# Mixing the second relational layer's matrices: which engine does which unit, and when its chunks are loaded

## The chip, the core and the metric

The kernel runs on one core of a Trainium2 chip. Its engines work in parallel, each through its own list of instructions, and wait for each other on semaphores: TensorE (PE, matrix products), VectorE (DVE), ScalarE (ACT), GpSimd (POOL), and SyncE (SP), which here only issues transfers. SBUF is the on-chip memory of 128 partitions; PSUM takes TensorE's results. The metric is the time of one execution in microseconds (us).

## What is computed

A graph of 1250 nodes with 512 features goes through four attention and MLP blocks and then through three graph layers. The change touches the last of these parts:

```python
# L1: alpha = x @ wc; beta = x @ wn; mean of beta over neighbours; sum of both
# L2, twice (basis1, then basis2):
def rgcn_gate_layer(x, row, col, edge_type, basis, att, gate_w, root, bias):
    w = jnp.einsum('rb,bio->rio', att, basis)      # att (2, 30), basis (30, 512, 512)
    x_j = x[col]
    for r in range(2):
        gate = jax.nn.sigmoid(x_j @ gate_w[r, :, 0])
        msgs.append(gate[:, None] * x_j @ w[r])
    msg = jnp.where((edge_type == 0)[:, None], msgs[0], msgs[1])
    return segment_sum(msg, row) + x @ root + bias
# L3: two SAGE layers of the same kind
```

The line that matters is the first one: for each of the two relations r, a 512 x 512 matrix is the weighted sum of 30 basis matrices.

## The kernel before

The nodes lie in T = 10 tiles of 125 rows. After the four blocks the kernel is written out by hand, stage by stage, and every engine has the same stages in its program:

- **beta1**: ten products of a node tile with a 512 x 512 matrix (`products`, eight matmuls each), each result split in two pieces by ACT (high part) and DVE (low part, `split_rows`).
- **mean1 / self1**: per tile a gather (`gather`: 20 matmuls of edge counts with all ten tiles' pieces) and one product. DVE adds both to x and takes the tile's statistics. POOL makes the reciprocal deviation (`tile_powers`).
- **msg 0,r** and **agg 0,r** for the relations r = 0, 1 of layer 0: ten products, split as above, then ten gathers. With r = 0 a gather also has the product with the root matrix.
- **msg 1,r** and **agg 1,r** of layer 1, then the SAGE stages.

The products and gathers take turns in five PSUM banks (`POST_BANKS`), so PE can be at most five results ahead of the engine that frees them.

The matrices of layer 1 are mixed while the stages up to `agg 0,1` run. They are w[0] (relation 0) and w[1] (relation 1), called `mixed[1][r]`. The work is cut in 120 units, one for each of 30 bases b and 4 row groups k (u = 4b + k). A unit reads one chunk of 128 x 512 numbers from HBM into a ring of three buffers, `ring[u % 3]`, named basis in the profile. DVE's `mix(n)` does the next n units: two instructions each (L1089, or L1087 for b = 0), accumulator r += att[r, b] * chunk, and then increments `basis_used`. SP's loop at L571 issues chunk n once `basis_used` has reached n - 2. Both queues are in order: a DVE instruction that waits for its chunk holds all that stands behind it, splits and adds included.

Before that loop SP issues the root matrix into w[2] (L560), the coefficients (L561), the two mixed matrices of layer 0 from their place in HBM (L564) and the gate rows (L566). At the same place POOL issues ct2 (L712) and adds a bias to all of x (`add_bias`, L695). Later POOL subtracts ct2 from ct in ten instructions (L719), after which ACT may convert the counts for `agg 0,0`, and adds another bias. PE may not start layer 1 before `mixed_ready`, which DVE gives behind unit 119.

## Time and profile before

| | before |
|---|---|
| median of 3 runs | 3251.54 us (3250.66 to 3256.28) |
| the profiled execution | 3254.82 us |
| its span (first to last instruction) | 3253.1 us |
| PE busy | 2931.6 us, 90% of the span |
| DVE busy | 1850.8 us, 57% |
| POOL busy | 899.4 us, 28% |
| mean granted TensorE clock | 0.952 of full speed |

PE is busy in most of the span, and where it isn't, some other engine or a transfer decides. The stages that the change touches lie between 2437 and 2820 us of the span. The shares over the whole span say little about them, so the views below are of this stretch.

### The profile page before, as it was taken

The page shows a single profiled execution, that of the slowest core. Times are in us where ns is not written, and L with a number is a line of the kernel's source. Part 1 is how long each engine was busy: PE and PEld are TensorE (multiplying, and loading weights), DVE is VectorE, ACT ScalarE, POOL GpSimd, SP SyncE. Part 2 cuts the span into 40 slices and gives each one's busy share as a digit, 9 for nine tenths or more (in the row PEclk, how much of TensorE's full clock was granted, in tenths as well). Part 3 has the DMA queues.
Part 4 walks back from the last instruction along what each step waited for, and adds up shares of the span by engine and source line. Part 5 has one row for each costly group of instructions (what it writes and reads, how often), then busy time and mean ns, then how long its engine had stood idle before and what let it go on. Part 6 is the DMA issues. An engine that isn't in the chain of part 4 may idle for free.

```text
span 3253.1 us, 32006 instructions
## 1 busy us (share of the span) xinstructions
PE 2931.6 (90%) x11830; PEld 1903.3 (59%) x11830; DVE 1850.8 (57%) x3327; ACT 793.8 (24%) x1145; POOL 899.4 (28%) x730
## 2 busy tenths in 40 slices
PE   5978389999899999889999979999977889999999
PEld 1345257777556777546777545777633545566555
DVE  9999345554765554855455764555674888603111
ACT  1154232222221222221222311222311112313221
POOL 6622122334222334221334320334511310000100
PEclk9989689999999999989999999999988989999999
DMA  3000200000310000310000230000144135101001
GB/s 78 1 1 1 93 7 14 1 27 14 107 46 13 1 27 13 95 59 13 1 27 1 67 99 13 1 26 1 51 126 140 51 105 151 52 13 65 13 0 32
DMA packets 69063, 133.70 MB, mean 41 GB/s; under 512 B 10804, under 2 KB 11195, under 8 KB 68908
## 3 DMA queue, kind: packets, MB, share of 16 engines
q1 hardware_dynamic: 63372, 119.62, 12.3%
q0 software_dynamic: 5536, 12.03, 1.1%
q8 instruction: 95, 1.56, 0.2%
q14 instruction: 60, 0.49, 0.1%
HBM read 120.70 MB, written 10.92 MB: 40 GB/s over the span
## 4 chain that ended last, share of the span: by engine, by line
PE 74%; DVE 13%; issue 4%; DMA 3%; DVEq 2%; ACT 1%; POOLq 1%; POOL 1%; SPq 0%; ACTq 0%
PE ps L1484 12%; PE ps L1596 10%; PE ps L1707 9%; PE ps L1736 9%; PE ps L1475 7%; PE ps L1634 4%; PE ps L1569 3%; PE ps L1584 3%; PE ps L1586 3%; PE ps L1587 3%; PE ps L1585 3%; PE ps L1437 2%; PE ps L1728 2%; PE ps L1501 2%; DMA lite_ring<-in_basis 2%
## 5 line engine op out<-in xcount | busy, mean ns | idle before, releaser
L687 POOL TENSOR_TENSOR pacc<-pacc,prob 125x628 f32<-125x628 f32 (+1 forms) x288 | 406.5, 1411 | 383.2 <-DVE prob L1013 383.2
L1484 PE MATMUL ps<-yT,w 128*128 128x416 f32 (+1 forms) x1152 | 438.2, 537 | 15.1 <-DVE qk_lo L957 7.8
L1596 PE MATMUL ps<-prob,big 125*128 125x314 f32 x1280 | 392.6, 428 | 4.6 <-DVE prob L1013 4.6
L966 DVE CUSTOM_DVE_ANT_0 ps<-ps,typed 125x628 f32<-125x628 f32 x320 | 260.1, 823 | 232.4 <-PE ps L1569 232.4
L1307 ACT ACTIVATE prob<-ps 125x628 f32<-125x628 f32 x320 | 221.9, 693 | 632.5 <-PE ps L1587 632.5
L1736 PE MATMUL ps<-pieces,counts_r 125*125 125x512 f32 x1400 | 353.9, 407 | 2.1 <-DVEq L1109 2.1
L1484 PEld LDWEIGHTS ps<-yT,w 128*128 128x128 f32 x1152 | 226.7, 198 | 201.3 <-issue 189.5
L1013 DVE SCALAR_TENSOR_TENSOR prob<-prob,typed 125x628 f32<-125x628 f32 x320 | 259.9, 812 | 124.0 <-ACT prob L1307 124.0
L1736 PEld LDWEIGHTS ps<-pieces,counts_r 125*125 125x125 f32 x1400 | 257.2, 186 | 79.6 <-issue 17.4
L1584 PE MATMUL ps<-qk_hi 128*125 128x314 f32 x640 | 294.9, 461 | 0.0
L1596 PEld LDWEIGHTS ps<-prob,big 125*128 125x128 f32 x1280 | 228.5, 190 | 60.4 <-DVE prob L1013 9.3
L1040 DVE SCALAR_TENSOR_TENSOR lite_acc<-lite_ring,att_w,lite_acc 128x512 f32<-128x512 f32 x232 | 198.7, 898 | 45.0 <-DMA lite_ring<-in_basis 35.7
L651 POOL TENSOR_TENSOR rstd<-var,mhalf 125x1 f32<-125x1 f32 x110 | 70.2, 639 | 547.2 <-DVE var L919 547.0
L957 DVE SCALAR_TENSOR_TENSOR qk_lo<-ps,bcol,qk_hi 128x416 fp32r<-128x416 f32 (+1 forms) x96 | 62.2, 651 | 254.7 <-ACT qk_hi L1269 254.7
L1475 PE MATMUL ps<-w,big 128*125 128x512 f32 x320 | 153.8, 628 | 54.9 <-DVE x L1055 52.0
L1586 PE MATMUL ps<-qk_hi,qk_lo 128*125 128x314 f32 x640 | 198.3, 310 | 0.0
L1587 PE MATMUL ps<-mrow,ones_r 128*125 128x314 f32 x640 | 198.3, 310 | 0.0
L1585 PE MATMUL ps<-qk_lo,qk_hi 128*125 128x314 f32 x640 | 198.1, 310 | 0.0
L683 POOL TENSOR_TENSOR pacc<-prob,zcol 125x628 f32<-125x628 f32 (+1 forms) x32 | 39.3, 1228 | 571.6 <-DVE prob L1013 571.6
L1089 DVE SCALAR_TENSOR_TENSOR w<-basis,att_w,w 128x512 f32<-128x512 f32 x232 | 175.1, 796 | 16.7 <-DMA basis<-in_basis 5.3
L1437 PE MATMUL ps<-onehot_src,onehot_dst 128*125 128x512 f16 x708 | 147.6, 354 | 31.7 <-DVE onehot_src L888 31.4
L1634 PE MATMUL ps<-w,oT 128*125 128x512 f32 x320 | 172.8, 625 | 0.6 <-DVE x L1000 0.6
(210 smaller groups left out, 4612.5 us busy)
## 6 DMA issues: line engine op xcount, KB each, us to landing
lite_ring<-in_basis SPq DMA_DIRECT2D x120, 256.0 KB, 2.6
basis<-in_basis SPq DMA_DIRECT2D x120, 256.0 KB, 2.6
w<-in_m_w SPq DMA_DIRECT2D x8, 1024.0 KB, 6.6
w<-in_wk SPq DMA_DIRECT2D x5, 1024.0 KB, 5.6
oT<-in_cw SPq DMA_DIRECT2D x9, 512.0 KB, 7.7
w<-in_wv SPq DMA_DIRECT2D x4, 1024.0 KB, 5.4
w<-in_wq SPq DMA_DIRECT2D x4, 1024.0 KB, 6.1
w<-in_wo SPq DMA_DIRECT2D x4, 1024.0 KB, 5.4
```

Of the source, the lines that this page charges most:

```text
L687: nc.gpsimd.tensor_tensor(pacc[:, c0:c0 + nn], pacc[:, c0:c0 + nn], prob[:, n % 3, p0:p0 + nn], ALU.add).then_inc(psum_done, 1)
L966: V.tensor_tensor_reduce(out=score_ps(s.slot), in0=score_ps(s.slot), in1=in_quarters(mneg[:, t, c0:c0 + HALF]), scale=1.0, scalar=-BIG, op ...
L1475: last = mm(lin_ps(job, P, D), lhs[:, k, t * P:(t + 1) * P], weight[:, k, :], start=(k == 0), stop=(k == KD - 1))
L1484: last = mm(lin_ps(job, 128, nn), weight[:, k, m * 128:(m + 1) * 128], lhs[:, k, c0:c0 + nn], start=(k == 0), stop=(k == KD - 1))
L1584: mm(o, hi[:, 1, rows], hi[:, 0, cols], start=True, stop=False)
L1585: mm(o, hi[:, 1, rows], lo[:, 0, cols], start=False, stop=False)
L1586: mm(o, lo[:, 1, rows], hi[:, 0, cols], start=False, stop=False)
L1587: last = mm(o, ones_r[:, 0:P], mrow[:, cols], start=False, stop=True)
L1596: last = mm(o_halves[:, b, :], vrow[:, t, h * DH:(h + 1) * DH], prob[:, n % 3, b * QUARTER:(b + 1) * QUARTER], start=(t == 0), stop=(t == ...
L1634: mm(lin_ps(job, P, D), oT[:, t * P:(t + 1) * P], w[0][:, h, :], start=True, stop=True).then_inc(lin_full, 1)
L1707: last = mm(post_ps(job, P, D), lhs[:, k, t * P:(t + 1) * P], weight[:, k, :], start=(k == 0), stop=(k == KD - 1))
L1736: last = mm(post_ps(job, P, D), counts_r[:, slot, k, :], pieces[:, piece, k, :], start=(self_ is None and k == 0 and piece == 0), stop=(k ...
```

## The change

Three things change.

1. **SP's order.** The chunks of the ring come directly behind the coefficients. The gate rows are issued before chunk 6, the two mixed matrices of layer 0 before chunks 10 and 14, the root matrix before chunk 18. On POOL, ct2 is issued when the last product of beta1 is there, behind the first bias.
2. **How many units where.** Per tile: 1 in beta1, 1 in mean1 (was 2), 1 in msg 0,0, 6 in agg 0,0 (was 5), 1 in msg 0,1, 2 in agg 0,1.
3. **Shared units.** In agg 0,0 every second unit (kind S, the others are kind D), and in agg 0,1 every unit, is shared, 50 in all: DVE does relation 0's half alone and increments `basis_used`. POOL then scales the chunk in its ring buffer, in place, and adds it to relation 1's accumulator (`mix_shared`). SP may reuse that buffer when POOL is done (`basis_shared`). DVE waits for POOL where the next whole unit of the same k needs the accumulator. PE waits for all 50 before layer 1.

```diff
+MIX_STEPS = (("beta1", "D"), ("mean1", "D"), ("msg0", "D"), ("agg0", "SDSDSD"), ("msg1", "D"), ("agg1", "SS"))
+def plan_mix():
+    units, shared = [], {}
+    for name, kinds in MIX_STEPS:
+        for t in range(T):
+            for kind in kinds:
+                if kind == "S":
+                    shared[len(units)] = len(shared) + 1
+                units.append(name)
+    return units, shared
...
             sp.wait_ge(blk_done, 2)
-            sp.dma_start(w[2][:], a["wk"][BLOCKS].rearrange("(k p) n -> p k n", p=128)).then_inc(root_in, 16)
             sp.dma_start(att_w[:].rearrange("p r b -> p (r b)"), a["att"][2 * BASES:].partition_broadcast(128)).then_inc(att_in, 16)
-            sp.wait_ge(mixed_out, 16 * BLOCKS)
-            for r in range(2):
-                sp.dma_start(mixed[0][r], mixed_d[r, :, :].rearrange("(k p) n -> p k n", p=128)).then_inc(mixed_in, 16)
-            sp.wait_ge(gate_rows_out, 64)
-            sp.dma_start(gate_row[0], gate_rows_d[0, :, :].partition_broadcast(P)).then_inc(gate_rows_in[0], 16)
             for n in range(BASES * KD):
                 b, k = n // KD, n % KD
+                if n == 6:
+                    sp.wait_ge(gate_rows_out, 64)
+                    sp.dma_start(gate_row[0], gate_rows_d[0, :, :].partition_broadcast(P)).then_inc(gate_rows_in[0], 16)
+                if n in (10, 14):
+                    r = (n - 10) // 4
+                    sp.wait_ge(mixed_out, 16 * BLOCKS)
+                    sp.dma_start(mixed[0][r], mixed_d[r, :, :].rearrange("(k p) n -> p k n", p=128)).then_inc(mixed_in, 16)
+                if n == 18:
+                    sp.dma_start(w[2][:], a["wk"][BLOCKS].rearrange("(k p) n -> p k n", p=128)).then_inc(root_in, 16)
                 if n >= 3:
                     sp.wait_ge(basis_used, n - 2)
+                    if n - 3 in SHARED:
+                        sp.wait_ge(basis_shared, SHARED[n - 3])
                 sp.dma_start(ring[n % 3][:], a["basis2"][b, k * 128:(k + 1) * 128, :]).then_inc(basis_in[n % 3], 16)
...
+            def mix_shared(name):
+                for u in (u for u in SHARED if MIX_AT[u] == name):
+                    b, k = u // KD, u % KD
+                    pool.wait_ge(basis_in[u % 3], 16 * (u // 3 + 1))
+                    pool.wait_ge(basis_used, u + 1)
+                    acc = mixed[1][1][:, k, :]
+                    nc.gpsimd.tensor_scalar(ring[u % 3][:], ring[u % 3][:], att_w[:, 1, b:b + 1], None, ALU.mult)
+                    nc.gpsimd.drain()
+                    nc.gpsimd.tensor_tensor(acc, acc, ring[u % 3][:], ALU.add)
+                    nc.gpsimd.drain().then_inc(basis_shared, 1)
...
-            nc.gpsimd.dma_start(ct2[:], count_rows(ct2_d)).then_inc(ct2_in, 16)
             pool.wait_ge(post_in, 16)
             add_bias(brow, 0, T)
+            pool.wait_ge(post_full, g["beta1"][-1].full)
+            nc.gpsimd.dma_start(ct2[:], count_rows(ct2_d)).then_inc(ct2_in, 16)
...
             add_bias(brow, 2, 2 * T)
+            mix_shared("agg0")
             late_load(w[2][:], matrix("root2"), g["agg", 0, 0][-1], pw_in)
             pool.wait_ge(agg_ready, 1)
             nc.gpsimd.dma_start(gate_row[1], gate_rows_d[1, :, :].partition_broadcast(P)).then_inc(gate_rows_in[1], 16)
+            mix_shared("agg1")
...
                     dve.wait_ge(basis_in[u % 3], 16 * (u // 3 + 1))
-                    for r in range(2):
+                    earlier = [SHARED[v] for v in range(k, u, KD) if v in SHARED]
+                    if u not in SHARED and earlier:
+                        dve.wait_ge(basis_shared, earlier[-1])
+                    for r in range(1 if u in SHARED else 2):
...
-                mix(1)
                 tile_shift(POST_NORM[NORM2], t)
...
-                        mix(5)
+                        mix(6)
...
                     pe.wait_ge(mixed_ready, 1)
+                    pe.wait_ge(basis_shared, len(SHARED))
```

The order of the instructions shows it at three places. First SP's transfers from the end of the four blocks on, before the change:

```order
L557 DMA mixed_d<-lite_acc 128x2x512
L560 DMA w<-in_wk 128x4x512
L561 DMA att_w<-in_att 128x60
L564 DMA big<-mixed_d 128x4x512 x2
L566 DMA big<-gate_rows_d 125x1024
L571 DMA basis<-in_basis 128x512 x120
```

And with the change (the loop's line is now L594):

```order
L575 DMA mixed_d<-lite_acc 128x2x512
L578 DMA att_w<-in_att 128x60
L594 DMA basis<-in_basis 128x512 x6
L583 DMA big<-gate_rows_d 125x1024
L594 DMA basis<-in_basis 128x512 x4
L587 DMA big<-mixed_d 128x4x512
L594 DMA basis<-in_basis 128x512 x4
L587 DMA big<-mixed_d 128x4x512
L594 DMA basis<-in_basis 128x512 x4
L589 DMA w<-in_wk 128x4x512
L594 DMA basis<-in_basis 128x512 x102
```

The big transfers have moved from ahead of the first chunk to between the first 18 chunks. Second, DVE in two successive tiles of agg 0,0, before:

```order
L1159 TENSOR_TENSOR agg<-ps,brow 125x512
L1089 SCALAR_TENSOR_TENSOR w<-basis,att_w,w 128x512 x10
L1159 TENSOR_TENSOR agg<-ps,brow 125x512
L1089 SCALAR_TENSOR_TENSOR w<-basis,att_w,w 128x512 x10
L1106 SCALAR_TENSOR_TENSOR pieces<-ps,gate,pieces 125x512
```

And with the change:

```order
L1198 TENSOR_TENSOR agg<-ps,brow 125x512
L1129 SCALAR_TENSOR_TENSOR w<-basis,att_w,w 128x512 x9
L1198 TENSOR_TENSOR agg<-ps,brow 125x512
L1129 SCALAR_TENSOR_TENSOR w<-basis,att_w,w 128x512 x9
L1146 SCALAR_TENSOR_TENSOR pieces<-ps,gate,pieces 125x512
```

A tile now has nine mixing instructions for six units where it had ten for five. Third, POOL from the subtraction of ct2 on, before:

```order
L719 TENSOR_TENSOR typed<-typed,ct 125x1250 x10
L695 TENSOR_TENSOR x<-x,brow 125x5120
L701 DMA w<-in_root 128x4x512
L724 DMA brow<-gate_rows_d 125x1024
L701 DMA w<-in_W_l 128x4x512
```

With the change the same place begins as follows, and the last two of these rows (one unit) come 30 times before the next transfer:

```order
L754 TENSOR_TENSOR typed<-typed,ct 125x1250 x10
L718 TENSOR_TENSOR x<-x,brow 125x5120
L738 TENSOR_SCALAR basis<-basis,att_w 128x512
L740 TENSOR_TENSOR w<-w,basis 128x512
```

POOL had nothing to compute between the second bias and the end of the layer. Now it has 100 instructions of 128 x 512 numbers there, 60 of them in agg 0,0, and each unit's second one reads what the first wrote.

## Rows read from the trace of the kernel before

**Rows 1.** The page's head line.
```profile
span 3253.1 us, 32006 instructions
```

**Rows 2.** The chain that ended last, 2250 to 3254: start, us, what.
```profile
2441.88 28.96 DMA basis<-in_basis
...
2578.69 28.14 POOLq L720
```

**Rows 3.** Timeline of PE, 2430 to 2500: start, us, line; in brackets idle before.
```profile
2438.97 13.90 PE L1707 MATMUL ps<-agg,yT 128*125 128x512 f32 x32
2472.77 15.95 PE L1707 MATMUL ps<-agg,yT 128*125 128x512 f32 x32 [19.91 <-DVE pieces L1103]
...
2495.82 3.60 PE L1707 MATMUL ps<-agg,yT 128*125 128x512 f32 x8
```

**Rows 4.** Timeline of DVE in beta1.
```profile
2470.93 0.88 DVE L1087 TENSOR_SCALAR w<-basis,att_w 128x512 f32<-128x512 f32 x2 [27.69 <-DMA basis<-in_basis]
...
2489.73 0.69 DVE L1103 TENSOR_TENSOR pieces<-ps,pieces 125x512 fp32r<-125x512 f32 x1
...
2492.09 0.69 DVE L1103 TENSOR_TENSOR pieces<-ps,pieces 125x512 fp32r<-125x512 f32 x1
```

**Rows 5.** Timeline of SP's transfers at the end of the blocks.
```profile
2437.44 0.46 SPq L560 DMA_DIRECT2D w<-in_wk  x1
...
2441.88 257.11 SPq L571 DMA_DIRECT2D basis<-in_basis  x76
```

**Rows 6.** Timeline of POOL, the two biases.
```profile
2442.76 11.01 POOL L695 TENSOR_TENSOR x<-x,brow 125x5120 f32<-125x5120 f32 x1
...
2606.95 11.00 POOL L695 TENSOR_TENSOR x<-x,brow 125x5120 f32<-125x5120 f32 x1 [0.29 <-issue]
```

**Rows 7.** Timeline of DVE beside POOL's 9.91 us instruction from 2345.68 on.
```profile
2345.75 10.14 DVE L1038 TENSOR_SCALAR lite_acc<-lite_ring,att_w 128x512 f32<-128x512 f32 x1
```

**Rows 8.** DVE's groups by form, 2578 to 2620: count, busy us, mean ns.
```profile
L1089 DVE SCALAR_TENSOR_TENSOR w<-basis,att_w,w 128x512 f32<-128x512 f32 x6 | 15.5, 2624 | 0.3
...
L1106 DVE SCALAR_TENSOR_TENSOR pieces<-ps,gate,pieces 125x512 fp32r<-125x512 f32 x2 | 1.5, 751 | 10.5 <-ACT pieces L1366 10.3
```

**Rows 9.** POOL's L719 alone, 2578 to 2607: min/median/max ns.
```profile
L719 POOL TENSOR_TENSOR typed<-typed,ct x10: 2536/2985/3069, 2578.7 to 2604.1; 125x1250 f16<-125x1250 f16 x10
```

**Rows 10.** POOL's L631 alone (min/median/max), L683 by form, whole span.
```profile
L631 POOL COPY typed<-run x59: 696/978/1218, 140.0 to 338.4; 125x625 int32 x59
...
L683 POOL TENSOR_TENSOR pacc<-prob,zcol 125x628 f32<-125x628 f32 x16 | 19.7, 1232 | 546.9 <-DVE prob L1013 546.9
```

**Rows 11.** Timeline of DVE, first tile of agg 0,0, splits of msg 0,1.
```profile
2643.92 0.69 DVE L1159 TENSOR_TENSOR agg<-ps,brow 125x512 f32<-125x512 f32 x1 [2.98 <-PE ps L1736]
2644.53 7.54 DVE L1089 SCALAR_TENSOR_TENSOR w<-basis,att_w,w 128x512 f32<-128x512 f32 x10
...
2729.91 0.75 DVE L1106 SCALAR_TENSOR_TENSOR pieces<-ps,gate,pieces 125x512 fp32r<-125x512 f32 x1
...
2752.05 0.75 DVE L1106 SCALAR_TENSOR_TENSOR pieces<-ps,gate,pieces 125x512 fp32r<-125x512 f32 x1
```

**Rows 12.** The page's transfers: KB each, us from issue to landing.
```profile
basis<-in_basis SPq DMA_DIRECT2D x120, 256.0 KB, 2.6
```

**Rows 13.** Timeline of DVE, two adds of agg 0,1.
```profile
2771.76 0.69 DVE L1115 TENSOR_TENSOR agg<-agg,ps 125x512 f32<-125x512 f32 x1
...
2777.45 0.69 DVE L1115 TENSOR_TENSOR agg<-agg,ps 125x512 f32<-125x512 f32 x1
```

**Rows 14.** Timeline of PE: agg 0,0 begins, msg 0,1 begins, layer 1 begins.
```profile
2635.64 3.60 PE L1728 MATMUL ps<-w,yT 128*125 128x512 f32 x8
...
2716.49 34.50 PE L1707 MATMUL ps<-big,yT 128*125 128x512 f32 x80
...
2809.83 9.52 PE L1707 MATMUL ps<-w,big 128*125 128x512 f32 x16 [7.53 <-DVEq L1093]
```

**Rows 15.** One stretch: us, busy of PE, PEld, DVE, ACT, POOL, PEclk, DMA share, GB/s.
```profile
2610.00:2618.00 8.00, 6.61 (x8) 2.47 (x8) 7.86 (x2) 2.74 (x5) 7.95 (x1) 0.58 0.00 0
```

More of the change, by code:

```diff
@@ L450, in build @@
         basis_used = sem("basis_used")
+        basis_shared = sem("basis_shared")
         xout_ready = sem("xout_ready")
```

1 line of the change is left out of this document (added).

## The prediction

> **What bounds the kernel now.** I began with the page's head [rows 1] and the chain that ended last, cut to the stretch from 2250 us on. From 2437 us almost every piece of it is PE, with two long strangers [rows 2]: 28.96 us of waiting for the first chunk of the ring, and 28.14 us behind POOL's subtraction of ct2. Then I read the timelines of the engines around each of them.
>
> *Stall A, end of beta1.* PE makes four products in 13.90 us (3.43 us each), stands idle for 19.91 us, and does the last four in 15.95 us [rows 3]. It lacks a PSUM bank, which DVE's second split would free, and DVE stands in the first unit's wait, 27.69 us, until the chunk is there at 2470.93 [rows 4]. SP had issued the root matrix at 2437.44 and four big transfers behind it, and reached the first chunk at 2441.88 [rows 5]. The chunk queued behind some 6 MB, ct2 among them.
>
> *Stall B, msg 0,0.* ACT may not convert counts until POOL has subtracted ct2. The change touches nothing on this path: last add of mean1, statistics, POOL.
>
> *The mixing, agg 0,0 to agg 0,1.* PE needs 8.09 us for a tile of agg 0,0 (2635.64 to 2716.49, ten tiles), while DVE needs 8.27: 0.69 for the add and 7.54 for five units [rows 11, 14]. DVE is 13 us behind when it comes to the first split of msg 0,1 (2729.91). In agg 0,1 it takes 5.69 us per tile [rows 13]. PE begins layer 1 at 2809.83 after a wait of 7.53 us for DVE's last unit [rows 14]. So in this stretch the mixing is the bound, by a little, and whatever it costs more is paid by PE.
>
> **The change, part by part.**
>
> *1. Chunks first: -24.5 us.* SP now reaches chunk 0 about 3 us earlier, ahead of all big transfers. It lands in about 3 us (0.33 for the issue and 2.6 to landing, [rows 12]; SP's issues are short, [rows 5]). DVE isn't free to use it, though. POOL's bias, 11.01 us long [rows 6], starts some 2 us earlier than before, at about 2440.5, since ct2's issue no longer stands ahead of it. DVE's scaling of a chunk can't run beside it: in the blocks the same kind of instruction took 10.14 us beside a long POOL instruction [rows 7]. So unit 0 ends at about 2452.4. The second split follows at 2452.5, just when PE is through with its sixth product (2438.97 + 13.90 = 2452.87). Splits then follow each other every 1.78 us (three units of b = 0: 0.69 + 0.88 + 0.2) and 2.36 us (five later ones, [rows 4]), the last one at 2469.6. PE's four remaining products end at 2453.2 + 13.7 = 2466.9, and its first gather (4.65 us) at 2471.5 instead of 2495.82 to 2496. That is -24.5 us, and the low-clock part of the old restart is in it. The gate rows between chunks 5 and 6, and a mixed matrix ahead of chunk 10, cost nothing: DVE has over a microsecond per product to spare in beta1, and in mean1 there is one unit in 8.5 us. If that cover were gone, each would cost what 1 MB takes beyond a chunk, a few us. ct2 has mean1's 85 us to land in.
>
> *2. One unit less per tile of mean1: 0.* PE bounds mean1. DVE's idle time there grows. Stall B stays as it is, only 24.5 us earlier.
>
> *3. agg 0,0 with shared units: +41 us.* By DVE's own work the tile would be cheap: 0.69 + 3 x 0.77 + 3 x 1.53 = 7.6 us, below PE's 8.09. What decides is the loop around the three buffers. Follow four units from an S half on DVE:
> - POOL makes its part: the scaling, a drain, the add, a drain. The trace has no scaling of 128 x 512 f32. Its copy of 625 numbers took 0.696 at least [rows 10], 0.57 for 512; its two-operand instructions need 2.15 ns a number (11.01 for 5120, [rows 6]), 1.10. I take 0.70, near the copy, since both read one operand. The add: 1.232 for 628 [rows 10] gives 1.00, the bias 1.10, so 1.05. Two drains and the hand-over: no row, 0.15 each and 0.05, between 0 and 0.6 together. Sum 2.10.
> - SP issues the chunk that reuses the buffer, three units on, a D unit: 0.33 + 2.6 = 2.93. Before, three units took 4.6 us per buffer, of which 1.53 for the unit and 2.93 for the load, so there was 0.1 to spare and no wait [rows 11].
> - DVE does that D unit, 1.53, and behind it the next S half, 0.77.
>
> 7.3 us for four units is 11.0 us for the six of a tile. Now the contention. Beside POOL's ten subtractions, DVE's mixing instruction took 2.62 us on average instead of 0.75, while one with an operand in PSUM kept its 0.75 [rows 8]. POOL's own went from 2.536 to 2.985 at the median [rows 9]. So the two take turns, POOL loses 0.45 to each of DVE's, and DVE waits for the rest of POOL's. In the loop POOL's two instructions run while DVE has a D unit, +0.9, and the awaited D unit meets some of POOL's, +0.2 (bounds 0 and 1.75, both its instructions waiting in full; low, since POOL's work for the unit before is then mostly over). 8.4 us for four units, **12.7 us per tile**.
>
> In before's clock, the first split of msg 0,1 then comes at 2643.92 + 127 = 2770.9 instead of 2729.91: +41. The nine splits behind it take 22.1 us before (to 2752.05, [rows 11]) and as long after, PE being five products ahead.
>
> *4. agg 0,1: +1 us.* DVE's own part falls to some 4.2 us and PE needs 5.08. POOL needs 2 x 2.1, and 0.45 for each of the four instructions of DVE (two halves, two logits) that come between: 6.0. I take 5.7 as before, and 1 us for POOL's last unit, for which PE waits now. Bounds -5 (PE decides: 0.6 in each of nine tiles) and +4.
>
> *5. PE's clock: +1 us.* The granted clock was 0.58 while eight matmuls took 6.61 us after stall B [rows 15] (3.43 at full clock). That is the 1.2 GHz level, and PE had been idle. PE will now stand idle for several us before each of the later products of msg 0,1, so one or two of these run slowly, up to 3 us, mostly beneath DVE's splits. The stall that goes in A gives its own slow part back, counted there.
>
> Everything else (POOL's root2, issued behind the 30 units of agg 0,0 but needed only in layer 1; the gate rows of layer 1) has tens of us of cover. The root matrix comes 30 us before its use.
>
> **Sum**: -24.5 + 41 + 1 + 1 = +18.5 on the profiled execution's 3254.8, so 3273. That execution is 3.3 us above the median of the runs shown, so I predict a median of **3270 us**.
>
> **The rivals.** With X for the tile of agg 0,0, the difference is 10X - 86 (the first split) - 24.5 + the last two terms. It changes sign at X = 10.9.
> - *No contention in the loop*: DVE's and POOL's turns fall beside each other by the waits themselves. X is 10.5 (POOL's short ends) to 11.3, and agg 0,1 is bound by PE (-5): -9 to -1, so 3242 to 3250 in the median. For it: both engines wait for chunks a good part of the time. Against: D units are twice as long as the gaps. Chance 0.18.
> - *Faster, the loop is hidden*: POOL's share would have to fit beside the load. PE's pace would need 5.4 us for four units, and load, D unit and S half alone are 5.2. It pays -24.5 and -5.5 in agg 0,1 in full, 3221 us, and it decides wherever X is below 10. For it: DVE's sum of 7.6 us, and 13 us of lag that would be worked off. Chance 0.10.
> - *Every instruction held in full, and POOL slow*: a DVE instruction holds POOL for its whole 0.75, the scaling takes 1.10 and drains 0.3. X is 14.5 to 15, agg 0,1 +5: over +40, so 3291 to 3300. The skill's rule above is on this side, but alone it doesn't reach it. Chance 0.10.
> - *Chunks first brings little*: the bias's 11 us (part 1) is already the price of this; if chunk 0 came only behind the write of lite_acc, it would still land within it. With it shifted by 3 us the sum is +21. Inside the forecast.
>
> **How the numbers follow.** The forecast (X from 11.3 to 14.5, +3 to +40) has 0.62. A measurement tells some 0.2%, 6.5 us, from no change. Of the forecast 0.59 is slower by more, 0.03 within. Of the uncontended case 0.10 is within, 0.08 faster. With the hidden and the slow case: slower 0.69, same 0.13, faster 0.18. The range goes from X = 10.5 to 14.5, 3240 to 3292, and leaves out most of the hidden and of the slow case, 0.18.
>
> **What the profile will show.** PE's idle time at the end of beta1 below 2 us, and DVE's first scaling some 9 us long beside the bias. Adds of agg 0,0 (L1198) 12.7 us apart, DVE waiting for chunks, L1129 on average 0.9 us or more there, POOL's unit 2.9 us from scaling to scaling's end. PE idle for over 30 us in msg 0,1, where it had none. Layer 1 starts about 18 us later. I am wrong if the adds stand under 10.9 us apart, or if POOL's unit takes under 1.8 us in all.

## The result and the profile after

| | before | after |
|---|---|---|
| median of 4 runs | 3253.31 us (3250.66 to 3256.28) | 3298.73 us (3297.8 to 3304.49) |
| the profiled execution's span | 3253.1 us | 3296.1 us |
| POOL busy | 899.4 us | 1048.3 us |
| mean granted TensorE clock | 0.952 | 0.950 |

The ratio after to before is 1.0143, 95% interval 1.0125 to 1.0161: the change makes the kernel 45 us slower. The forecast was 3270 us, with a range up to 3292. The direction came as forecast, and the size lies above the range.

The ratio differs from 1 by more than the noise, though by less than 2%. The two profiled executions are compared stage by stage. The anchor is the start of the third product of beta1, where the long row of products begins: 2438.97 us before [rows 3], 2431.36 after. The change touches nothing that PE waits for ahead of this point, and it still lies 7.6 us earlier in the trace of after. Over all profiled executions of this study it lay between 2430.2 and 2442.5, so executions of one and the same part differ by that much. From the anchor to the end, after takes 864.7 us and before 814.1.

| stretch | before, us | after, us | difference | forecast |
|---|---|---|---|---|
| anchor to the first product of self1 | 56.85 | 32.30 | -24.55 | -24.5 |
| mean1 and self1 | 76.20 | 76.20 | 0 | 0 |
| to the first product of agg 0,0 (stall B in it) | 63.62 | 63.09 | -0.5 | 0 |
| agg 0,0 to the first split of msg 0,1 | 94.27 | 149.19 | +54.9 | +41 |
| the ten splits of msg 0,1 | 22.14 | 22.67 | +0.5 | 0 |
| last split to layer 1 | 57.78 | 78.16 | +20.4 | +1 (and +1 for the clock) |
| layer 1 to the end | 443.3 | 443.1 | -0.1 | 0 |
| sum | | | +50.6 | +18.5 |

Less the 7.6 us ahead of the anchor, that is the +43.0 between the two spans. The forecast is missed by 32 us: 14 of them in the row of agg 0,0, 18 in the one up to layer 1.

**Stall A is gone.** PE in the stretch of [rows 3], on its timeline (start, us, what; idle time before in brackets):

```profile
2431.36 27.82 PE L1746 MATMUL ps<-agg,yT 128*125 128x512 f32 x64
2458.61 5.21 PE L1775 MATMUL ps<-pieces,counts_r 125*125 125x512 f32 x20
2463.66 3.60 PE L1746 MATMUL ps<-agg,yT 128*125 128x512 f32 x8
```

The eight products now run in one piece, where [rows 3] has 19.91 us of idle time behind the first four. DVE's first unit stands on its timeline as

```profile
2435.85 8.41 DVE L1127 TENSOR_SCALAR w<-basis,att_w 128x512 f32<-128x512 f32 x2 [0.21 <-DMA basis<-in_basis]
2444.37 0.69 DVE L1143 TENSOR_TENSOR pieces<-ps,pieces 125x512 fp32r<-125x512 f32 x1
```

and POOL's bias of 11.03 us began at 2432.54. Two scalings that take 0.88 us together elsewhere take 8.41 here and end with the bias. The chunk is there in time, and the second split doesn't hold PE.

**agg 0,0 goes at the pace of the ring.** Its adds on DVE, in one row of the view of that line, and DVE's and POOL's groups of 2611 to 2752 us (count, busy us, mean ns, idle before and its releaser):

```profile
L1198 DVE TENSOR_TENSOR agg<-ps,brow x10: 691/692/694, 2611.2 to 2737.1; 125x512 f32<-125x512 f32 x10
```
```profile
L1129 DVE SCALAR_TENSOR_TENSOR w<-basis,att_w,w 128x512 f32<-128x512 f32 x90 | 82.6, 944 | 51.0 <-DMA basis<-in_basis 48.4
```
```profile
L738 POOL TENSOR_SCALAR basis<-basis,att_w 128x512 f32<-128x512 f32 x30 | 49.6, 1652 | 71.1 <-DVEq L1131 69.8 <-issue 1.3
L740 POOL TENSOR_TENSOR w<-w,basis 128x512 f32<-128x512 f32 x30 | 40.4, 1346 | 4.6 <-issue 4.6
```

Ten adds in 125.9 us are nine intervals of 13.98 us on average (they alternate between some 13 and some 15), where [rows 11] and [rows 14] had 8.27 and 8.09. DVE waits 48.4 us for chunks, and POOL 69.8 us for DVE, of which 27.59 lie ahead of its first unit (2612.80): neither engine is full. What closes the loop stands in the chain that ended last (start, us, what), here one turn of it, and the next one's begin:

```profile
2628.00 1.52 DVE w L1129
2631.21 1.61 POOLq L739
2632.94 1.60 POOLq L741
2634.61 2.54 DMA basis<-in_basis
2637.18 1.59 DVE w L1129
```

DVE's whole unit, the relation-0 half of the next, POOL's scaling and add, then the load into the buffer that POOL gave free, and DVE's next whole unit: 9.18 us for four units, 13.8 for the six of a tile. (Three turns beside it in the same chain took 8.5, 8.7 and 10.4 us. The longest has the add of a tile in it.) Two of POOL's units on its timeline show their parts:

```profile
2616.84 1.56 POOL L738 TENSOR_SCALAR basis<-basis,att_w 128x512 f32<-128x512 f32 x1 [0.27 <-issue]
2618.56 1.28 POOL L740 TENSOR_TENSOR w<-w,basis 128x512 f32<-128x512 f32 x1 [0.15 <-issue]
2622.12 1.56 POOL L738 TENSOR_SCALAR basis<-basis,att_w 128x512 f32<-128x512 f32 x1 [2.29 <-DVEq L1131]
```

**PE pays in msg 0,1 and at the end of agg 0,1.** PE's waits between 2330 and 2880 us (in total, times, longest; of the second row 20.7 us are the two waits in msg 0,0, where before had 19.92):

```profile
PE ps L1746 <- DVE agg L1198: 33.7, 4, 9.3
PE ps L1746 <- DVE pieces L1146: 30.3, 3, 16.6
...
PE ps L1746 <- issue: 16.6, 1, 16.6
PE ps L1576 <- ACT py L1382: 11.2, 6, 1.9
```

Two of the later products of msg 0,1 and the first of layer 1 on PE's timeline:

```profile
2696.68 5.66 PE L1746 MATMUL ps<-big,yT 128*125 128x512 f32 x8 [9.30 <-DVE agg L1198]
2709.88 5.89 PE L1746 MATMUL ps<-big,yT 128*125 128x512 f32 x8 [7.53 <-DVE agg L1198]
...
2852.97 9.44 PE L1746 MATMUL ps<-w,big 128*125 128x512 f32 x16 [16.63 <-issue]
```

PE has finished its ten gathers and stands for 16.63 us. The view names only "issue" for it, but POOL's last add ended 0.15 us before PE went on:

```profile
2851.56 1.26 POOL L740 TENSOR_TENSOR w<-w,basis 128x512 f32<-128x512 f32 x1 [0.15 <-issue]
```

Why that is so late is on POOL's timeline in agg 0,1:

```profile
2813.96 1.81 POOL L738 TENSOR_SCALAR basis<-basis,att_w 128x512 f32<-128x512 f32 x1 [0.27 <-issue]
2815.92 1.29 POOL L740 TENSOR_TENSOR w<-w,basis 128x512 f32<-128x512 f32 x1 [0.15 <-issue]
2817.48 1.72 POOL L738 TENSOR_SCALAR basis<-basis,att_w 128x512 f32<-128x512 f32 x1 [0.27 <-issue]
2819.35 1.51 POOL L740 TENSOR_TENSOR w<-w,basis 128x512 f32<-128x512 f32 x1 [0.15 <-issue]
2821.12 1.80 POOL L738 TENSOR_SCALAR basis<-basis,att_w 128x512 f32<-128x512 f32 x1 [0.26 <-issue]
```

Here POOL never waits for anyone: two units from 2813.96 to 2821.12 are 7.16 us, and DVE's adds of agg 0,1 stand 7.16 us apart as well, where [rows 13] had 5.69. The +20.4 us splits in -0.5 ahead of the first add, +13.3 in the nine intervals, and +7.7 behind the last add. DVE ended its last half at 2846.34, and POOL was nearly two units behind and needed 6.5 us more.

### The profile page after: what moved, and what is told of

Read it like the earlier page. It is cut to its first block, busy times and chain, and to the rows that moved or that the text cites. A ratio compares the mean times of both kernels' runs of the same rounds, so it can differ in the third digit from the quotient of the medians.

```text
span 3296.1 us, 32258 instructions
## 1 busy us (share of the span) xinstructions
PE 2935.7 (89%) x11830; PEld 1901.6 (58%) x11830; DVE 1852.2 (56%) x3277; ACT 793.1 (24%) x1145; POOL 1048.3 (32%) x830
## 4 chain that ended last, share of the span: by engine, by line
PE 72%; DVE 12%; POOLq 4%; issue 4%; DMA 3%; ACT 2%; DVEq 1%; POOL 1%; SPq 0%; ACTq 0%
PE ps L1523 12%; PE ps L1635 10%; PE ps L1746 9%; PE ps L1514 7%; PE ps L1775 7%; PE ps L1673 4%; PE ps L1608 3%; PE ps L1623 3%; PE ps L1625 3%; PE ps L1624 3%; PE ps L1626 3%; PE ps L1476 2%; PE ps L1540 2%; DMA lite_ring<-in_basis 2%; DVE onehot_src L925 2%
## 5 line engine op out<-in xcount | busy, mean ns | idle before, releaser
L1129 DVE SCALAR_TENSOR_TENSOR w<-basis,att_w,w 128x512 f32<-128x512 f32 x182 | 164.7, 934 | 79.0 <-DMA basis<-in_basis 70.3
```

## The experiments

Two theories were set against each other. The first (A): the changed order gains some 24 us by itself, and the shared units lose the rest by the time for which a buffer is held (DVE's half, POOL's unit, load), lengthened by turns at SBUF. The rival: POOL's work in itself, or its contention with DVE, is the cost, and the hold is not. For each run the time from the anchor to the end is given against before's 814.1 us ("by the trace"), besides the medians, since the part ahead of the anchor varies by up to 12 us. "By the trace" is one execution of each kernel. Most stages behind the anchor repeat within 1 us where the program is the same, but not all: from the first product of self1 to the first of agg 0,0 experiments 1 and 11 run the same program and took 140.8 and 145.5 us. There PE's granted clock was 1.00 behind the second split of msg 0,0 in the one and 0.82 in the other. So differences of up to some 5 us by the trace are not shown by it alone. X is the interval of agg 0,0's adds.

**1. The order alone** (e1_chunks_first). All units whole, as many per tile as before:

```diff
-MIX_STEPS = (("beta1", "D"), ("mean1", "D"), ("msg0", "D"), ("agg0", "SDSDSD"), ("msg1", "D"), ("agg1", "SS"))
+MIX_STEPS = (("beta1", "D"), ("mean1", "DD"), ("msg0", "D"), ("agg0", "DDDDD"), ("msg1", "D"), ("agg1", "DD"))
...
                 tile_statistics(t)
+                mix(1)
...
-                        mix(6)
+                        mix(5)
...
-                    pe.wait_ge(basis_shared, len(SHARED))
```

> The new order of the transfers alone (SP's and POOL's), units as before (2 in mean1, 5 in agg 0,0), none shared. Theory A (the order is worth what the two traces show between the third product of beta1 and the first self product, 56.85 us against 32.30, and the loss is all in the shared units): -24.5 us against before, some 3229 us. Theory B (chunks between the big transfers cost something later, in mean1 or at the wait for the mixed matrices): less than 15 us gained.

Measured 3233.44 us against 3250.36, ratio 0.9939 (0.9922 to 0.9956). By the trace -23.8, X = 8.28. The order is worth some 24 us alone (by the ratio 20, from 14 to 25), and nearly all of it, 24.7, stands in the stretch from the anchor to the first product of self1.

**2. The shares with the old order** (e2_old_order). SP's root matrix, mixed matrices and gate rows again ahead of the first chunk, and ct2's issue ahead of the first bias; the rest as in the change.

```diff
             sp.wait_ge(blk_done, 2)
+            sp.dma_start(w[2][:], a["wk"][BLOCKS].rearrange("(k p) n -> p k n", p=128)).then_inc(root_in, 16)
...
+            sp.wait_ge(mixed_out, 16 * BLOCKS)
+            for r in range(2):
+                sp.dma_start(mixed[0][r], mixed_d[r, :, :].rearrange("(k p) n -> p k n", p=128)).then_inc(mixed_in, 16)
```

> The changed kernel with the transfers in their old order: units moved and shared as in the change. Theory A: the two parts add up, so 24.5 us above the changed kernel, some 3323 us (+70 on before). Theory B: the order and the sharing hang together (the gain of the order is partly lost to the later stage, which would have absorbed it), so less than 15 us above the changed kernel.

Measured 3325.72 us, ratio 1.0232 (1.0214 to 1.0249). By the trace +75.0, X = 14.00. The two parts add: -23.8 + 75.0 = +51.2, and the whole change has +50.6.

**3. Units moved, none shared** (e3_units_moved). Six whole units in agg 0,0 and one in mean1:

```diff
+MIX_STEPS = (("beta1", "D"), ("mean1", "D"), ("msg0", "D"), ("agg0", "DDDDDD"), ("msg1", "D"), ("agg1", "DD"))
...
-                    pe.wait_ge(basis_shared, len(SHARED))
```

> New order and the new numbers of units (1 in mean1, 6 in agg 0,0), but every unit whole, made by DVE. Theory A (the sharing costs, not the move): a tile of agg 0,0 is 0.69 + 6 x 1.53 = 9.9 us instead of 8.27, so +16 on the kernel with the order alone: some 3245 us, still below before. Theory B (moving a unit of each tile out of mean1 is what costs): 3275 us or more.

Measured 3240.77 us, ratio 0.9965 (0.9952 to 0.9978). By the trace -10.4, so the unit moved from mean1 costs 13.4 us on top of experiment 1, and that 50 units are shared the other 61. X is 9.80 in seven of the nine intervals and longer in two, 11.04 and 11.70, which stand here as DVE's adds:

```profile
2663.63 0.69 DVE L1198 TENSOR_TENSOR agg<-ps,brow 125x512 f32<-125x512 f32 x1
...
2673.43 0.69 DVE L1198 TENSOR_TENSOR agg<-ps,brow 125x512 f32<-125x512 f32 x1
...
2684.47 0.69 DVE L1198 TENSOR_TENSOR agg<-ps,brow 125x512 f32<-125x512 f32 x1
...
2696.17 0.69 DVE L1198 TENSOR_TENSOR agg<-ps,brow 125x512 f32<-125x512 f32 x1
```
```profile
2687.64 0.83 POOL L724 DMA_DIRECT2D w<-in_root  x1 [99.02 <-PE ps L1775]
```

POOL's 1 MB root matrix was issued at 2687.64 and took 6.3 us to land, so it was coming in during the second of the two, and chunks took up to 5.0 us then. The first lies ahead of it. One chunk took 4.3 us there, and the runs don't show why. The two together are 3.1 of the 13.4 us.

**4. POOL's part left out** (e6_no_pool). Without relation 1's half of the 50 units and all waits for it:

```diff
-                    if n - 3 in SHARED:
-                        sp.wait_ge(basis_shared, SHARED[n - 3])
...
-            mix_shared("agg0")
-            mix_shared("agg1")
...
-                        dve.wait_ge(basis_shared, earlier[-1])
...
-                    pe.wait_ge(basis_shared, len(SHARED))
```

> The changed kernel with POOL's part of the 50 shared units left out (relation 1's matrix lacks these terms), and nobody waits for it: DVE's own sum, with no hold of the buffers and no contention. Theory A: PE decides in agg 0,0 (8.09 us a tile) and in agg 0,1 (5.08), so -24.5 and some -6 more: 3222 us. A rival by which DVE's six units can't run at PE's pace even then, since a half unit leaves the loads too little time (three units in 3.8 us against the 2.93 of a load and 1.53 of a unit): a tile of 8.8 us or more, 3229 us or more.

Measured 3220.69 us, ratio 0.9901 (0.9876 to 0.9925). By the trace -33.8, X = 8.51. For this plan of units this is the floor: 10 us below the order alone. If POOL's work were free, the whole prize would be these 10 us. None of it comes from agg 0,0, where X stays above the 8.28 of experiment 1 and PE's 8.09 that theory A expected, even with no buffer held for POOL. Half of it is agg 0,1, whose adds stand 5.03 us apart instead of 5.58.

**5. POOL without its scaling** (e5_no_scaling). POOL adds the raw chunk.

```diff
-                    nc.gpsimd.tensor_scalar(ring[u % 3][:], ring[u % 3][:], att_w[:, 1, b:b + 1], None, ALU.mult)
-                    nc.gpsimd.drain()
```

> The changed kernel without POOL's scaling of the chunk (relation 1 gets the unscaled chunk): POOL's unit falls from 3.28 us (1.57 + 0.15 + 1.29 + 0.27) to 1.6. Theory A (the length of POOL's part, through the buffer it holds): the loop of four units gets 1.7 us shorter, 2.6 us per tile of agg 0,0, from 14.0 to 11.4, and agg 0,1 falls from 7.16 us per tile to PE's 5.08: about -26 and -20, so 3253 us. Rival (what costs is the turn-taking of DVE and POOL): only half of the 100 turns go, so about -20, 3279 us.

Measured 3259.72 us, ratio 1.0023 (1.0014 to 1.0033). By the trace +6.5, X = 11.25. A unit shorter by 1.8 us takes 2.7 off the tile, 1.5 turns of 1.8. In agg 0,1 the adds stand 6.07 us apart and not 5.08 as expected. That is 9 us in nine intervals, where the run came out 7 us above its expectation.

**6. POOL's work apart from the ring** (e7_pool_apart). In agg 0,0 POOL makes the same two instructions on a buffer of its own, and SP doesn't wait for it:

```diff
+                    scaled = big[:, 4096:4608] if name == "agg0" else ring[u % 3][:]
-                    nc.gpsimd.tensor_scalar(ring[u % 3][:], ring[u % 3][:], att_w[:, 1, b:b + 1], None, ALU.mult)
+                    nc.gpsimd.tensor_scalar(scaled, scaled, att_w[:, 1, b:b + 1], None, ALU.mult)
...
-                    nc.gpsimd.tensor_tensor(acc, acc, ring[u % 3][:], ALU.add)
+                    nc.gpsimd.tensor_tensor(acc, acc, scaled, ALU.add)
```

> In agg 0,0 POOL does its two instructions on a buffer of its own that no transfer writes (relation 1 lacks the chunks of these 30 units), and SP does not wait for it there; agg 0,1 as in the change. POOL's work and its turns with DVE stay, the hold of the chunk's buffer goes. Theory A, revised (the round trip chunk, DVE, POOL, SP, load decides in agg 0,0): the tile falls from 14.0 us to what POOL's three units and DVE's turns need, 10.5 to 11.5, so -25 to -35: some 3268 us. Rival (POOL's throughput with the turns decides in agg 0,0 too): the tile stays at 13 us or more, 3288 us or more.

Measured 3274.66 us, ratio 1.0072 (1.0055 to 1.0088). By the trace +23.4, X = 11.41. POOL's groups in agg 0,0:

```profile
L740 POOL TENSOR_SCALAR big<-big,att_w 128x512 f32<-128x512 f32 x30 | 56.4, 1881 | 37.7 <-DVEq L1133 33.6 <-issue 4.1
L742 POOL TENSOR_TENSOR w<-w,big 128x512 f32<-128x512 f32 x29 | 41.8, 1441 | 4.4 <-issue 4.4
```

The 37.7 us have 27.49 ahead of the first unit. With the hold gone, 2.6 us of X go, and the next bound is near. It is DVE itself, which now hardly waits:

```profile
L1131 DVE SCALAR_TENSOR_TENSOR w<-basis,att_w,w 128x512 f32<-128x512 f32 x90 | 100.9, 1147 | 5.9
```

In the chain that ended last a tile is DVE's nine instructions and its add, and nothing else. The instructions take 1147 ns on average, where experiment 1 has 748, since POOL works beside them nearly without a pause (three units with their gaps are some 11 us of POOL per tile too). So the rival has a part: the turns at SBUF, 3.6 us per tile here, would keep agg 0,0 well above PE's pace even if no buffer were held.

**7. The buffer freed early** (e8_early_free). POOL scales out of the ring into a buffer of its own; SP may reload as soon as that is done.

```diff
+                    scaled = big[:, 4096:4608] if name == "agg0" else ring[u % 3][:]
-                    nc.gpsimd.tensor_scalar(ring[u % 3][:], ring[u % 3][:], att_w[:, 1, b:b + 1], None, ALU.mult)
-                    nc.gpsimd.drain()
-                    nc.gpsimd.tensor_tensor(acc, acc, ring[u % 3][:], ALU.add)
+                    nc.gpsimd.tensor_scalar(scaled, ring[u % 3][:], att_w[:, 1, b:b + 1], None, ALU.mult)
+                    nc.gpsimd.drain().then_inc(basis_scaled, 1)
+                    nc.gpsimd.tensor_tensor(acc, acc, scaled, ALU.add)
```

> The changed kernel, with the scaled chunk of agg 0,0 written to a buffer of its own, so that SP may reuse the ring buffer after the scaling, not after the add. The same arithmetic and instructions. Theory A: the loop of four units gets 1.44 us shorter (0.15 and 1.29), so 2.1 us per tile: -21, some 3278 us. Rival (throughput and turns): no change, 3299 us.

Measured 3278.66 us, ratio 1.0073 (1.0053 to 1.0094). By the trace +24.3, X = 11.57. POOL does all its work here, DVE's instructions are as long as in the change (957 ns), and 2.4 us per tile go with the shorter hold alone. POOL waits 0.75 us for DVE in nearly every unit, so its own pace isn't the bound. That falls against the rival: the work is the same, and only the hold changed.

**8. The second bias behind the mixing** (e9_late_bias). Experiment 1, and:

```diff
-            add_bias(brow, 2, 2 * T)
...
+            pool.wait_ge(mixed_ready, 1)
+            add_bias(brow, 2, 2 * T)
```

The bias behind the subtraction of ct2 now waits for the end of the mixing.

> The order alone, as in e1, and POOL's second bias moved from behind the subtraction of ct2 to the point where the mixing is done. In the trace of the changed kernel DVE's first mixing instruction of msg 0,0 takes 7.7 us beside that bias, and PE waits 4.2 us for the split behind it. If that collision is what holds PE there: 3 to 6 us below e1, some 3225 us. If the bias only collides with other work in its new place: same as e1.

Measured 3229.66 us, ratio 0.9934 (0.9917 to 0.9950). By the trace -26.3, 2.5 below experiment 1, a little less than expected. The wait of PE behind the second split, 3.59 us in experiment 1, is gone in the trace, so the collision was there. That it makes the kernel faster isn't shown: the two ratios can't be told apart, and 2.5 us is within what one execution differs from another there.

**9. The coefficient as a broadcast row** (e10_multiply_by_row). The change, with POOL's scaling as a product of two tensors:

```diff
-                    nc.gpsimd.tensor_scalar(ring[u % 3][:], ring[u % 3][:], att_w[:, 1, b:b + 1], None, ALU.mult)
+                    nc.gpsimd.tensor_tensor(ring[u % 3][:], ring[u % 3][:], att_w[:, 1, b:b + 1].to_broadcast([128, D]), ALU.mult)
```

> The changed kernel with POOL's scaling written as a product of two tensors, the coefficient being broadcast along the row (the same arithmetic). Theory A (POOL's part was mis-sized by its scaling, 1.57 us where the bias, a sum with a broadcast row, took 1.10 for 512 numbers and a sum with a broadcast column 0.95 to 1.0): the scaling falls to 1.0, 0.5 us less in a unit, so 0.8 us per tile of agg 0,0 and 1.0 per tile of agg 0,1: -18, 3281 us. Rival (POOL's second instruction and its turns set the pace, or the form makes no difference): 3299 us.

Measured 3296.17 us, ratio 1.0139 (1.0118 to 1.0160). By the trace +44.3, X = 13.88. A miss: the scaling itself did get shorter, from a median of 1.566 to 1.042 us (view of its line, min/median/max):

```profile
L738 POOL TENSOR_TENSOR basis<-basis,att_w x50: 1040/1042/1599, 2613.7 to 2844.9; 128x512 f32<-128x512 f32 x50
```

But the groups of agg 0,0 show where it went again, DVE's instruction from a mean of 944 ns to 1127 and POOL's add from 1346 to 1460:

```profile
L1129 DVE SCALAR_TENSOR_TENSOR w<-basis,att_w,w 128x512 f32<-128x512 f32 x90 | 99.1, 1127 | 32.4 <-DMA basis<-in_basis 29.7
```
```profile
L740 POOL TENSOR_TENSOR w<-w,basis 128x512 f32<-128x512 f32 x30 | 43.8, 1460 | 4.4
L738 POOL TENSOR_TENSOR basis<-basis,att_w 128x512 f32<-128x512 f32 x30 | 32.9, 1096 | 83.1 <-DVEq L1131 83.1
```

**10. Both** (e11_row_and_free). Experiments 7 and 9 together.

```diff
+                    nc.gpsimd.tensor_tensor(scaled, ring[u % 3][:], att_w[:, 1, b:b + 1].to_broadcast([128, D]), ALU.mult)
+                    nc.gpsimd.drain().then_inc(basis_scaled, 1)
+                    nc.gpsimd.tensor_tensor(acc, acc, scaled, ALU.add)
```

> Both mends at once: the scaling as in e10, and the scaled chunk of agg 0,0 in a buffer of its own as in e8. Theory A: POOL then needs 3 x 2.9 us and the turns in a tile of agg 0,0, about 10.5 us, and 6.2 in one of agg 0,1: some 3259 us, so sharing stays slower than the order alone (3233) even so. Rival (sharing pays once its two costs are mended): 3233 us or less.

Measured 3284.31 us, ratio 1.0096 (1.0078 to 1.0114). By the trace +32.1, X = 12.70: worse than experiment 7 alone, against the expectation. DVE's mean is 1222 ns:

```profile
L1131 DVE SCALAR_TENSOR_TENSOR w<-basis,att_w,w 128x512 f32<-128x512 f32 x90 | 107.6, 1222 | 12.8 <-DMA basis<-in_basis 8.8
```

**11. One shared unit per tile** (e12_one_shared). Experiment 1 with one of five units of agg 0,0 shared. POOL is nearly idle then.

```diff
-MIX_STEPS = (("beta1", "D"), ("mean1", "D"), ("msg0", "D"), ("agg0", "SDSDSD"), ("msg1", "D"), ("agg1", "SS"))
+MIX_STEPS = (("beta1", "D"), ("mean1", "DD"), ("msg0", "D"), ("agg0", "SDDDD"), ("msg1", "D"), ("agg1", "DD"))
```

> The order alone, as in e1 (2 units in mean1, 5 in agg 0,0, 2 in agg 0,1), with only the first of the five units of each tile of agg 0,0 shared. POOL has 3.3 us of work in a tile, so its throughput can't be the bound, and DVE's own sum is 7.6 us. Theory A (the hold of one of three buffers: DVE does two whole units, 3.1 us, while POOL and the load take 3.3 + 2.9): a wait of 3.2 us in every tile, 10.8 us instead of 8.27, so +25 on e1: 3258 us. Rival (only POOL's throughput or the number of turns costs): PE's pace of 8.09 us, 3231 us.

Measured 3260.42 us, ratio 1.0020 (1.0009 to 1.0031). By the trace +10.5, X = 11.42, where all five units whole have 8.28. One tile on DVE's and then POOL's timeline:

```profile
2644.66 0.69 DVE L1199 TENSOR_TENSOR agg<-ps,brow 125x512 f32<-125x512 f32 x1
2645.27 2.71 DVE L1129 SCALAR_TENSOR_TENSOR w<-basis,att_w,w 128x512 f32<-128x512 f32 x3
2648.17 2.44 DVE L1129 SCALAR_TENSOR_TENSOR w<-basis,att_w,w 128x512 f32<-128x512 f32 x2 [0.19 <-issue]
2652.75 1.41 DVE L1129 SCALAR_TENSOR_TENSOR w<-basis,att_w,w 128x512 f32<-128x512 f32 x2 [2.15 <-DMA basis<-in_basis]
```
```profile
2646.21 2.10 POOL L738 TENSOR_SCALAR basis<-basis,att_w 128x512 f32<-128x512 f32 x1 [7.42 <-DVEq L1131]
2648.47 1.59 POOL L740 TENSOR_TENSOR w<-w,basis 128x512 f32<-128x512 f32 x1 [0.15 <-issue]
```

The shared half is done at about 2646.1, POOL at 2650.06, and the chunk that reuses the buffer is there at 2652.75. DVE has used up the other two buffers by 2650.6 and stands for 2.15 us. The two units that it does meanwhile are longer by turns, but they aren't what it waits for. One shared unit per tile costs 3.1 us, 31 in ten tiles, although it takes 0.7 us of work off DVE. The chain that ended last goes through it in every tile: half, POOL's unit, load, then DVE's last two units, add and next half. The expectation had 3.3 us for POOL's unit. It took 4.0 with its drains (2.10 + 1.59 + 0.3), which is the 0.6 us by which X lies above the 10.8 that was expected.

**12. Units where DVE is idle** (e13_idle_units). Experiment 8, with two units ahead of msg 0,1 (behind the gates) and none in the last tile of agg 0,1:

```diff
+            mix(2)
...
-                        mix(2)
+                        mix(2 if t < T - 1 else 0)
```

> e9 (new order, bias behind the mixing, nothing shared) with two units taken from the last tile of agg 0,1 and done behind the gates of layer 0, where DVE waits some 10 us for the counts. Their four instructions take turns with the subtraction of ct2 (3 us each), so the first split comes about 1 us later, and layer 1 starts 3 us earlier: 2 us below e9, some 3228 us. If the waiting time was no real slack: same as e9 or above.

Measured 3228.00 us, ratio 0.9926 (0.9907 to 0.9944). By the trace -25.9 against -26.3: not to be told from experiment 8. Layer 1 starts 5.8 us earlier from the anchor, and the rest takes 6.2 longer. Most of that is one wait: the late bias begins when the mixing is done, and DVE's gate instruction beside it took 11.50 us instead of 0.70. In experiment 8 it did too, but PE didn't wait for what stands behind it. Here DVE's last add of agg 0,1 does, and PE waits 5.25 us:

```profile
2776.50 11.50 DVE L1166 CUSTOM_DVE_ANT_0 ps<-py,brow 125x512 f32<-125x512 f32 x1 [0.25 <-issue]
```
```profile
2790.51 1.09 PE L1579 MATMUL ps<-ident,py 125*128 125x125 f32 x4 [5.25 <-ACT py L1385]
```

So the idle time was real slack, and the late bias took its gain back. Another place for the bias wasn't tried.

**13. POOL only writes** (e14_write_only). In agg 0,0 POOL's two instructions are three fills of a buffer of its own, about as long in all, with the same waits. Relation 1's half is left out there.

```diff
+                    if name == "agg0":
+                        nc.gpsimd.memset(big[:, 4096:5120], 0.0)
+                        nc.gpsimd.drain()
...
+                        nc.gpsimd.drain().then_inc(basis_shared, 1)
+                        continue
```

> The changed kernel; in agg 0,0 POOL's part of a shared unit is three settings of 128 x 1024 numbers to zero, each with its drain, in a region that nobody reads (relation 1 lacks these units): estimated 3.3 us, about the length of the real part, but POOL reads no SBUF. Everything waits as in the change. Theory A (length and hold set the tile, DVE's delays by POOL's reads only add to it): DVE's mixing instruction of agg 0,0 falls from 0.944 us on average to 0.75, and the tile from 13.98 to about 13.0 (3.3 + 0.05 + 2.93 + 1.53 + 0.77 for four units, 12.9 for six). Rival (the turns are the larger part of what the tile costs): 12 us or less at the same length.

One execution, 3288.0 us. By the trace +37.0, X = 12.86. DVE's group:

```profile
L1137 DVE SCALAR_TENSOR_TENSOR w<-basis,att_w,w 128x512 f32<-128x512 f32 x96 | 69.2, 749 | 57.1 <-DMA basis<-in_basis 54.1 <-POOLq L744 0.2 <-issue 0.2
```

DVE is undisturbed (749 ns; in [rows 11] ten took 7.54 us), and X still is 12.86. So the hold's length sets most of it, and the turns at SBUF are the other 1.1 us per tile.

**14. The scaling twice** (e15_scaled_twice). The add of agg 0,0 is replaced by a second scaling, which changes the result.

```diff
-                    nc.gpsimd.tensor_tensor(acc, acc, ring[u % 3][:], ALU.add)
+                    if name == "agg0":
+                        nc.gpsimd.tensor_scalar(ring[u % 3][:], ring[u % 3][:], att_w[:, 1, b:b + 1], None, ALU.mult)
```

> The changed kernel; in agg 0,0 POOL scales the chunk a second time instead of adding it (relation 1 lacks these units): POOL's part is 2 x 1.57 + 0.42 = 3.55 us instead of 3.28, and has no instruction with two tensors. Theory A2, from e10 (only POOL's two-tensor instruction makes DVE's mixing wait, its scaling by a column does not): DVE's mixing instruction falls to 0.75 us on average, and the tile to about 13.3. Rival (every POOL instruction that reads SBUF takes its turn): DVE's stays at 0.94 or more, and the tile goes to 14.2 or more.

One execution, 3294.09 us. By the trace +48.1, X = 13.94. DVE's mean:

```profile
L1132 DVE SCALAR_TENSOR_TENSOR w<-basis,att_w,w 128x512 f32<-128x512 f32 x88 | 70.8, 832 | 58.2 <-DMA basis<-in_basis 55.8 <-issue 0.2
```

832 ns lies between the two expected values, 0.75 and at least 0.94. One-operand scalings delay DVE less than adds do, but not by nothing.

**The loop, checked on all of them.** The prediction's loop is POOL's hold h, hand-over 0.05, load 2.93, and three DVE instructions d (a whole unit and a half), all times 1.5 for a tile. With h and d from each run's groups (h is the sum of POOL's means, each plus 0.15 for its drain, for as long as the buffer is held):

| kernel | h | d | loop x 1.5 | X measured |
|---|---|---|---|---|
| after | 3.30 | 0.944 | 13.7 | 13.98 |
| 9, broadcast row | 2.86 | 1.127 | 13.8 | 13.88 |
| 14, scaled twice | 3.60 | 0.832 | 13.6 | 13.94 |
| 13, only writes | 3.31 | 0.749 | 12.8 | 12.86 |
| 10, row and early | 1.47 | 1.222 | 12.2 | 12.70 |
| 7, early | 1.73 | 0.957 | 11.4 | 11.57 |
| 5, no scaling | 1.54 | 0.945 | 11.0 | 11.25 |

Nothing is fitted, though h and d are taken from the same traces as X. The formula is 0.1 to 0.5 us short over seven kernels. It leaves out DVE's add of a tile, which stands in the chain of the changed kernel in five of the nine intervals of agg 0,0, 0.4 us per tile. Experiment 6 isn't in the table, since DVE and not a held buffer is its bound. Whether a fourth buffer would open the loop wasn't tried. Experiment 7 has a region of that size to itself in agg 0,0, so there is room for one in this stage.

## Why the prediction was right in its direction and wrong in its size

1. *Chunks first: -24.5.* Right, to 0.05 us in the trace, closer than executions repeat, so that is luck in part, and confirmed alone in experiment 1. The first scaling beside the bias was 8.41 us long, "some 9" as predicted, the splits behind it stand 1.83 and 2.36 us apart, and PE's idle time is gone.
2. *One unit less in mean1: 0.* Right, 76.20 us both times. The move of the unit was costed at 0 on this side and within the +41 on the other. Experiment 3 shows what it costs with no unit shared: 13 us, two slow loads included.
3. *agg 0,0: +41 with X = 12.7.* This is the step that failed, in one term of its sum: the length of POOL's part, "Sum 2.10". It was built of 0.70 for the scaling, taken near the copy of [rows 10] "since both read one operand", 1.05 for the add and 0.35 for the rest. The scaling took 1.566 at the median, 2.2 times as much, the add 1.295, and the drains 0.15 each. With the hand-over that is 3.2 against 2.1. Its upper bound of 1.10 for the scaling was no bound either, because it came from instructions of another form.
   The term for contention was off the other way, and in its place: 1.1 us of each turn were expected, 0.9 of them as longer POOL instructions. Experiment 13 shows 1.1 us of each tile, so some 0.75 of each turn, and the groups put most of that on DVE: three instructions at 944 instead of 749 ns are 0.6, while POOL's two are some 0.15 longer than their medians. With 3.2 for 2.1 and 0.75 for 1.1 the predicted loop is 8.4 + 1.1 - 0.35 = 9.15, times 1.5 is 13.7, and the add that stands in the chain in half the tiles brings it close to the 13.98 that was measured. The forecast's mechanism was right: the ring closes the loop, and experiments 5, 7, 11 and 13 each changed one part of it and moved X as it says.
4. *agg 0,1: +1, bounds -5 and +4.* The same term once more, and here it cost more, 18 of the 32 us. With 2.1 a unit the sum was 6.0 a tile, and the prediction took 5.7. With 3.58 a unit and no gap POOL is itself the bound, 7.16 a tile, +13.3 in nine intervals. PE's wait for the last unit was put at 1 us, and +7.7 came, since POOL as the bound was nearly two units behind DVE at the end.
5. *PE's clock: +1.* Right as far as it can be seen. Four of the later products of msg 0,1 took 5.18 to 5.89 us instead of 3.60, with a granted clock of 0.63 to 0.71 in them, so partly at the lower level of 1.2 GHz, after 7.5 to 9.3 us of idle time each. DVE set the pace there, since PE waited for it again before the next product.

The rival that named "POOL slow" put the median at 3291 to 3300, and 3298.73 lies in that. One half of its reason was right, that POOL's instructions are long. The other, that every instruction is held in full, wasn't, since the turns were smaller than forecast. That its number came out is luck: X was below its 14.5 to 15, and agg 0,1 lost 20 us instead of its 5. Neither of the two signs that were to refute the forecast came (adds under 10.9 us apart, POOL's unit under 1.8). Of the signs for its size, POOL's unit was 3.15 us from the scaling's start to the add's end instead of 2.9, and layer 1 started 51 us later from the anchor instead of 18.

Two things weren't seen ahead. Shorter POOL instructions gain little if they take DVE's time instead. In experiment 9 h fell by 0.44, and three d rose by 0.55. Why a product with a broadcast row disturbs DVE more than a scaling, in numbers 1127 against 944 ns, the runs don't show; only that a pure write disturbs it not at all and a doubled scaling by 83 ns. And the prize was small from the start: experiment 4 puts it at 10 us beyond the new order, while one shared unit per tile costs 31 (experiment 11).

The best version is the new order with all units whole: experiments 1, 8 and 12, ratios 0.9939, 0.9934 and 0.9926, which the runs can't tell apart.

## What to carry to other kernels

Work that is split between two engines on one buffer holds that buffer for both of them and the load, one behind the other. With a ring of few buffers, count that loop first: the engines' busy times may both have room. Price an instruction on another engine by a row of that very form on that engine, and where there is none, let the upper bound reach well past the nearest form. Measure the order of transfers apart from the sharing of work: here one gained 24 us and the other lost three times that.

## What the runs showed of the hardware

- POOL's multiplication of 128 x 512 f32 numbers by one number per partition took 1.566 us, longer than its addition of two such tensors (1.295) and its product with the coefficient broadcast along the row (1.042). Its copy of 125 x 625 int32 had taken 0.696 at least [rows 10].
- Two POOL instructions with a drain between stand 0.15 us apart, and unit follows unit after 0.27.
- POOL's fill of 128 x 1024 f32 took 0.952 us and left DVE's two-operand instruction at 749 ns. Two scalings per unit made that 832, scaling and add 944 (1147 in experiment 6, where POOL hardly pauses), product and add 1127, and with the buffer freed early 1222. The Trainium skill, "SBUF — State Buffer", section "Who interferes with whom", says that a DVE instruction with two inputs in SBUF contends with a GpSimd instruction that reads SBUF, and not with one that only writes it. The trace agrees, by 832 ns and more against 749. The rule that the prediction took from the same section, the pair held for a whole instruction, would have made the turns longer than forecast, and they were shorter.
- While 1 MB came in by POOL's queue, a ring of 256 KB chunks slowed from 9.80 to 11.70 us per six chunks (experiment 3).
- Executions of the same part of the program, up to the anchor, differ by up to 12.3 us. From the anchor on most stages repeat within 1 us. The stretch with stall B in it differed by 4.7 us between experiments 1 and 11.
